# Linear attention between two LayerNorm half-steps on one Trainium2 core: gain, shift and output bias loaded as one row each and spread over the partitions by float32 products

## What is computed

```python
x = x + 0.5 * ffn(layernorm(x))        # LayerNorm half-step
x = x + attn(layernorm(x))             # attn: causal linear attention, 16 heads of 32
x = x + 0.5 * ffn(layernorm(x))        # the same half-step again
# attn: q, k, v = y@Wq.T, y@Wk.T, y@Wv.T; phi = elu + 1
#       S += phi(k) v^T; z += phi(k); out = (phi(q) S) / (phi(q) z + EPS); out @ Wo.T + bo
```

## Time and profile before

| what | us |
|---|---|
| three runs | 927.19, 929.17, 929.96 |
| median of the runs | 929.17 |
| profiled execution, first to last instruction (span) | 928.0 |
| PE busy | 895.7 |
| DVE busy | 832.5 |
| ACT busy | 753.6 |
| POOL busy | 705.9 |

### The profile page before, as it was taken

How to read it: one execution, slowest core, us unless ns; L and a number is a source line. 1 busy time by engine, 2 the same in 40 slices (tenths; PEclk the granted TensorE clock), 3 DMA queues, 4 the chain that set the end, 5 groups by cost and what they waited for, 6 DMA issues and landing times.

```text
span 928.0 us, 29932 instructions
## 1 busy us (share of the span) xinstructions
PE 895.7 (97%) x10252; PEld 525.3 (57%) x10252; DVE 832.5 (90%) x1537; ACT 753.6 (81%) x1301; POOL 705.9 (76%) x869
## 2 busy tenths in 40 slices
PE   3999999999999999999999999999999999999985
PEld 2555555655555655555565555565555566555562
DVE  6989889999999999999999999999999999999686
ACT  5888878888888888888888888888888888888672
POOL 3268777789777778877778977777887777887572
PEclk9999999999999999999999999999999999999998
DMA  7576798776677766768767667776667876766882
GB/s 249 137 147 134 144 182 159 143 145 150 146 167 158 157 139 151 150 149 179 156 137 149 147 147 169 158 156 138 152 147 153 175 157 137 149 129 124 155 138 68
DMA packets 421564, 139.80 MB, mean 151 GB/s; under 512 B 402576, under 2 KB 402832, under 8 KB 421520
## 3 DMA queue, kind: packets, MB, share of 16 engines
q1 hardware_dynamic: 404496, 106.73, 61.1%
q10 hardware_dynamic: 17024, 32.51, 10.5%
HBM read 21.76 MB, written 16.78 MB: 42 GB/s over the span
## 4 chain that ended last, share of the span: by engine, by line
PE 86%; DVE 4%; DMA 4%; issue 3%; ACT 1%; POOL 1%; SPq 0%; DVEq 0%; ACTq 0%; POOLq 0%
PE PJ L1596 48%; PE PJ L1701 17%; PE AV L1675 7%; PE SC L1648 6%; PE AV L1687 5%; PE AV L1672 2%; DMA AT<-ATTN 2%; DMA X<-in_L_attn_x_dram 1%; DMA shift<-in_L_ffn_ln_b_dram 1%; DVE AM L1166 1%; DMA KS<-KN 1%; DVE TP L1290 0%; ACT A L783 0%; POOL X1BO L433 0%; DVE X L1126 0%
## 5 line engine op out<-in xcount | busy, mean ns | idle before, releaser
L1596 PE MATMUL PJ<-wT,XT 128*128 128x512 f16 x2304 | 525.2, 380 | 0.2
L1596 PEld LDWEIGHTS PJ<-wT,XT 128*128 128x128 f16 x2304 | 217.5, 98 | 244.4 <-issue 3.6
L500 POOL TENSOR_TENSOR A<-AM,A 128x512 f16<-128x512 f32 x252 | 288.2, 1163 | 31.3 <-ACT A L783 31.2
L1701 PE MATMUL PJ<-wT,AT 128*128 128x512 f16 x768 | 177.2, 380 | 1.0 <-DMA AT<-ATTN 0.9
L490 POOL TENSOR_SCALAR_AFFINE_SELECT AM<-AM 128x512 f32<-128x512 f32 x124 | 79.2, 638 | 114.3 <-ACT AM L770 114.3
L783 ACT ACTIVATE A<-AM 128x512 f16<-128x512 f32 x256 | 153.7, 632 | 13.7 <-POOL AM L490 10.1
L1675 PE MATMUL AV<-VN,A 128*128 128x33 f16 x3072 | 116.5, 178 | 0.0
L1701 PEld LDWEIGHTS PJ<-wT,AT 128*128 128x128 f16 x768 | 71.5, 98 | 79.5 <-DMA AT<-ATTN 2.5
L1672 PE MATMUL AV<-SS,QS 128*128 128x33 f16 x1024 | 111.8, 178 | 0.0
L1675 PEld LDWEIGHTS AV<-VN,A 128*128 128x128 f16 x3072 | 108.9, 96 | 3.8
L1166 DVE TENSOR_TENSOR AM<-SC,causal 128x512 f32<-128x512 f32 x132 | 90.0, 684 | 20.9 <-PE SC L1648 20.3
(11 more groups left out here) (113 smaller groups left out, 1521.0 us busy)
## 6 DMA issues: line engine op xcount, KB each, us to landing
out_dram<-Y ACTq DMA_DIRECT2D x31, 512.0 KB, 3.2
X<-in_L_attn_x_dram ACTq DMA_DIRECT2D x30, 512.0 KB, 3.4
X<-in_L_attn_x_dram SPq DMA_DIRECT2D x2, 512.0 KB, 8.0
A<-in_L_attn_Wk_dram SPq DMA_DIRECT2D x1, 1024.0 KB, 9.2
A<-in_L_attn_Wq_dram SPq DMA_DIRECT2D x1, 1024.0 KB, 11.5
QS<-in_L_attn_Wv_dram SPq DMA_DIRECT2D x1, 1024.0 KB, 15.6
XT<-XH SPq DMA_TRANSPOSE x64, 3.3
QS<-in_L_attn_Wo_dram SPq DMA_DIRECT2D x1, 1024.0 KB, 5.4
```

What stands on the lines that cost most here:

```text
L500: g.tensor_tensor(A[:, b, LO, hg], AM[:, k % 4], A[:, b, HI, hg], ALU.subtract).then_inc(a_lo.sem, 1)
L1596: ins = t_.matmul(PJ[b], XT[:, w, c, b * C:(b + 1) * C], wT[m_][:, m, c, :], start=(c, w, m) == todo[0], stop=(c, w, m) == todo[-1])
L1701: ins = t_.matmul(PJ[b], AT[:, b, w, c * C:(c + 1) * C], wT[3][:, m, c, :], start=(c, w, m) == todo[0], stop=(c, w, m) == todo[-1])
```

## The change

Gain, shift and bias are loaded as one row each to one partition, into parts of the tiles Y and X2 that nothing else uses yet. Three float32 products on PE, each of `ones_row` (1x128) with a row (1x512), write the three rows over all 128 partitions of three PSUM banks (SC0, SC1 and one of AV). DVE reads gain and shift out of PSUM as it halves them, and copies the bias (`whole_obias`, a new step). The bias is now loaded before the weights. The weight transposes that use these banks next wait until DVE has read them.

```diff
--- before.py
+++ after.py
@@ -139,6 +139,7 @@
         X2 = sb("X2", [P, BATCH, E])
         Y = sb("Y", [P, BATCH, E])
         raw2 = sb("raw2", [P, BATCH, 6])
+        rows = [Y[0:1, 0], Y[0:1, 1], X2[0:1, 0]]
         wsq = AM
 
         TP = [ps(f"TP{i}") for i in range(2)]
@@ -165,8 +166,10 @@
         wT_filled = sem("wT_filled")
         wT_hi = sem("wT_hi")
         wT_lo = sem("wT_lo")
+        row_spread = sem("row_spread")
         gain_scaled = sem("gain_scaled")
         shift_scaled = sem("shift_scaled")
+        obias_done = sem("obias_done")
         zeroed = sem("zeroed")
 
         x_loaded = [sem(f"x_loaded{p}") for p in range(2)]
@@ -269,15 +272,16 @@
                 sp.dma_start(X[:, i], x[:, i * C:(i + 1) * C, :].rearrange("b p e -> p b e")).then_inc(x_loaded[i], 16)
 
             load_x(0)
-            sp.dma_start(gain[:], ln_g.rearrange("(a n) -> a n", a=1).to_broadcast([P, E])).then_inc(gain_loaded, 16)
-            sp.dma_start(shift[:], ln_b.rearrange("(a n) -> a n", a=1).to_broadcast([P, E])).then_inc(shift_loaded, 16)
+            sp.dma_start(rows[0], ln_g.rearrange("(a n) -> a n", a=1)).then_inc(gain_loaded, 16)
+            sp.dma_start(rows[1], ln_b.rearrange("(a n) -> a n", a=1)).then_inc(shift_loaded, 16)
             def load_w(j):
                 m = W_ORDER[j]
                 sp.dma_start(wnat[m], weights[m].rearrange("(c p) e -> p c e", p=P)).then_inc(w_loaded[m], 16)
 
             def load_bias():
-                sp.dma_start(obias[:], attn_bo.rearrange("(a n) -> a n", a=1).to_broadcast([P, E])).then_inc(obias_loaded, 16)
-
+                sp.dma_start(rows[2], attn_bo.rearrange("(a n) -> a n", a=1)).then_inc(obias_loaded, 16)
+
+            load_bias()
             load_w(0)
             load_w(1)
             load_x(1)
@@ -353,7 +357,6 @@
 
             def opening():
                 early, first, second = ops(Step(0, -2)), ops(Step(0, -1)), ops(Step(0, 0))
-                load_bias()
                 early.turn_x(0)
                 early.turn_x(1)
                 load_w(3)
@@ -426,7 +429,7 @@
                         if not PROJECT:
                             return
                         if not ATTEND:
-                            pool.wait_ge(obias_loaded, 16)
+                            pool.wait_ge(obias_done, 1)
                         pool.wait_ge(*x1_done.upto(n, 1))
                         if FINISH:
                             pool.wait_ge(*x2_done.upto(back, 1))
@@ -1024,12 +1027,16 @@
             dve.wait_ge(zeroed, 1)
 
             def half_gain():
-                dve.wait_ge(gain_loaded, 16)
-                v.tensor_scalar(gain[:], gain[:], 0.5, None, ALU.mult).then_inc(gain_scaled, 1)
+                dve.wait_ge(row_spread, 1)
+                v.tensor_scalar(gain[:], SC[0][:], 0.5, None, ALU.mult).then_inc(gain_scaled, 1)
 
             def half_shift():
-                dve.wait_ge(shift_loaded, 16)
-                v.tensor_scalar(shift[:], shift[:], 0.5, None, ALU.mult).then_inc(shift_scaled, 1)
+                dve.wait_ge(row_spread, 2)
+                v.tensor_scalar(shift[:], SC[1][:], 0.5, None, ALU.mult).then_inc(shift_scaled, 1)
+
+            def whole_obias():
+                dve.wait_ge(row_spread, 3)
+                v.tensor_copy(obias[:], AV2[:, 1]).then_inc(obias_done, 1)
 
             def row_sums(j):
 
@@ -1371,6 +1378,7 @@
                 early.front_mean(1)
                 half_gain()
                 half_shift()
+                whole_obias()
                 early.front_gain(0)
                 early.front_gain(1)
                 early.front_x1(0)
@@ -1562,10 +1570,16 @@
             t_ = nc.tensor
             pe.wait_ge(consts_done, 1)
 
+            def spread_row(i):
+                pe.wait_ge((gain_loaded, shift_loaded, obias_loaded)[i], 16)
+                t_.matmul((SC[0], SC[1], AV2[:, 1])[i][:], ones_row[:], rows[i], start=True, stop=True).then_inc(row_spread, 1)
+
             def w_turn(j, c):
 
                 m, k = W_ORDER[j], j * GROUPS + c
                 pe.wait_ge(w_loaded[m], 16)
+                if 2 <= k < W_REUSE:
+                    pe.wait_ge((gain_scaled, shift_scaled, obias_done)[k - 2], 1)
                 if k >= W_REUSE:
 
                     pe.wait_ge(wT_lo, k - len(spare) + 1)
@@ -1733,6 +1747,9 @@
 
             def opening():
                 first, second = ops(Step(0, -1)), ops(Step(0, 0))
+                spread_row(0)
+                spread_row(1)
+                spread_row(2)
                 w_turn(0, 0)
                 w_turn(0, 1)
                 turn_norm(0)
```

## The result

The changed kernel takes 932.20 us (median of 6 runs, 931.42 to 934.91), against 928.87 us for the kernel before in 6 runs (926.73 to 929.96): ratio 1.0039, 95% interval [1.0023, 1.0056]. It is slower by 3.3 us, where 929.7 us and no change were forecast, and 0.7 us outside the range. The profiled execution of the change took 931.42 us for a span of 929.7 us; so 1.7 us lie outside a span here, and the span of 928.0 us before stands for 929.7 us, not the 929.2 us that the prediction read it as.

A forecast was written before the change was run, and what follows sets the result against it. PE was taken to bound the loop, so only the opening counted: front_gain 1.4 us later, partly absorbed by DVE's waits, leaves 0.5; 928.0 + 0.5 = 928.5, plus 1.17 outside the span, gives 929.7 us. Range 927.1 to 931.5 us.

The forecast's parts named there:

- the rows land: Opening: the row loads of gain, shift and bias arrive at 4.5 us, between a floor of 4.3 and a ceiling of 6.1.
- a product takes: Opening, PE: each of three float32 spreading products takes 1.75 us, 5.25 us together, with DVE waiting behind them.
- `front_gain` at 10.40: Opening, DVE: front_gain starts at 10.5 in place of 9.12 us, 1.4 us later, behind products and bias copy.
- L1038's counterpart: Opening, DVE: the step that waited for ACT's square of Wk stands ready at 14.4 us, 0.9 later than 13.55.
- the wait for chunk 2: Opening, DVE: its 0.37 us wait for the load of x's chunk 2, before the statistics at 18.11 us, goes.
- ACT held by its own issue: Opening, ACT: the square of Wk waits for ACT's issue of chunk 2, itself behind front_gain, and starts at 12.0 us.
- Wk early to no use: Opening, loads: Wk lands 2 to 4 us earlier, shortening the path only as far as front_gain is not later.
- the opening 0.59 us later: End of opening: the first weight transposes on PE, at 21.77 us before, start about 0.5 us later.
- rivals on the products' speed: Opening, PE: products of 1.04 us give 927.4 us (14 in 100); with half-speed clock stretch also gone, 925.8 (10 in 100).
- late rows: Opening, DVE's wait: rows at 6.1 us and products of 1.94 us each give 931.9 us, slower (8 in 100).
- The steady window: Mid-loop: in 100 us PE is busy 100.00 us and DVE 91.60, so the loop is PE's.
- the time outside the span: Whole kernel: the runs' median stands 1.17 us above the profiled span (929.17 - 928.0), added to the forecast.

The follow-up runs named there:

- e2_dve_late: Kernel before plus two memsets of unused tiles (some 1.3 us of DVE) behind half_shift, PE's list and loads unchanged: 931.70 us, ratio 1.0018.
- e4_bias_copy_late: Changed kernel with whole_obias moved on DVE from ahead of front_gain to behind the first half-step's result statistics: 931.34 us, ratio 1.0027 to the kernel before.
- h13_pad268: Kernel before plus 134 tiny products (268 idle instructions) at the head of PE's list: 932.31 us, ratio 1.0035.

## Why the prediction was wrong

Right, by its own steps: the rows land at 4.3 us (4.5); a product takes 1.7 us (1.75); `front_gain` at 10.40 (10.5); L1038's counterpart at 14.44 (14.4); the wait for chunk 2 gone; ACT held by its own issue and Wk early to no use; the opening 0.59 us later (0.5). The last is right for the one profile from which it was read. The transposes of the seven profiles with broadcast loads and no delay on DVE started at 20.9 to 21.8 us (median 21.19), those of the three with the change's order on DVE at 22.3 to 22.5 us, so the typical loss of the opening is nearer to 1.2 us, an estimate from these profiles: that 0.5 met 0.59 was in part luck. By the Trainium skill, "FP8 and Floating Point Precision", section TensorE Precision Notes, a float32 product goes in four passes, which with the earlier trace rows makes an estimate of 1.71 us; the measured 1.7 us agrees. The rivals on the products' speed and on late rows did not come true. The time, 932.2 us, is close to the 931.9 us of the last of them, by another path: its copy of the bias was to end at 12.7 us, and it ended at 10.5.

Wrong was a step of the first part: "The change puts nothing into it, so it can act only by the moment at which PE gets its unbroken work, and whatever the opening gains or loses moves the end by as much. So the sum is one of the opening alone." The change does put something into the early loop: 12 instructions in PE's list, which move the later fetches of instructions against the DMA transposes. The loop added 2.4 and 2.7 us in the two profiles, where the sum has nothing; 12 idle instructions alone added 2.8 us, 268 added 2.5 and 256 added 0.3. The late start that the change also brings can do the same (2.0 us in e2_dve_late), so how the loss of the change divides between its instructions and its delay is open. The steady window was rightly read; it says nothing of the stretch from 64 to 200 us, where PE waits for some of the transposes when they land 1.6 us late. The queue of instruction packets stood on the page of before (q8, 25 packets, 0.41 MB), and no term was made of it.

A smaller error: the time outside the span was taken as 1.17 us from a median of other executions; it is 1.7 us. And no term stands for the speed of TensorE behind the transposes: the twelfth product of the projection starts 2.9 to 4.4 us behind the first, differently in two profiles of one kernel (3.35 and 4.37 us for the change).

## To carry to other kernels

A loop that is full on average can still have early iterations in which a transfer lands just in time; look there, in unrolled code above all, for what any shift of a list can hit. When a small edit of the opening moves the time by more than its own offset, compare the same mark early and late in both traces, and run the kernel before with as many idle instructions on the engine as the edit added: if that alone shows the loss, what the edit computes is not its cause, and a pad may be the cure. Look at the same mark in two profiles of one kernel first, and compare from ahead of the first loss: here a loss at 52 us stood ahead of the first mark and made a pad look better than it was. Behind a row load, put each reader where it is first needed, so that products on PE run beside DVE's work and not ahead of it.

## What the runs showed of the hardware

- A transpose by DMA with one of PE's 16 KB instruction packets in flight (0.9 to 1.5 us on a single DMA engine) often lands 1.6 us later, in 129 of 276 cases: 6.1 in place of 4.4 us for KN.
- The time depends on the number of instructions of PE, by up to 3.1 us, though they are idle, and 256 more leave it as it was: 12 and 268 more are slow (932.22, 932.31 us), 48 stand between (930.07), 0, 112 and 256 are not slow (928.89, 927.97, 928.96). Other multiples of 256 were not run.
- TensorE's first float16 products, behind float32 transposes with waits between them, start 0.43 us apart and then 0.22 us apart. The switch came within the third to the tenth step in the 15 profiles, also between profiles of one kernel, and moved the twelfth product by up to 1.5 us. The record of the granted clock can read 1.00 all the while (e4_bias_copy_late).
- In the closing TensorE was granted 1.2 GHz for 3.4 us at a time at different places (865 and 903 us in the kernel before, 869 us in the change, 903.6 to 910.5 us in h13_pad268).
- The landing of the broadcast of shift differed between executions, 6.9 to 8.9 us in nine profiles with broadcast loads, while chunk 0 ahead of it landed at 4.2 to 4.5 us in all of them. The first profile of before (8.75) was among the late ones; so the opening's loss by the change is larger against the typical execution than the 0.6 us read from one pair.
